# Who evicts the keys, and ScalarE's order, in the 48 rounds of a decoder's cross-attention

## What is computed

```python
k = at @ Wk.T + bk ; v = at @ Wv.T + bv        # at: 1500 x 256 for each batch entry, 16 heads of 16
scores = clip(q @ k.T / 4, -50, 50)            # masked rows: -50
ctx = softmax(scores) @ v
```

## Time and profile before

| what | value |
|---|---|
| median of 3 runs | 502.4 us |
| the profiled execution, its own time | 503.83 us |
| its span, first to last instruction | 502.0 us |
| TensorE busy | 475.0 us (95%) |
| VectorE busy | 363.7 us (72%) |
| ScalarE busy | 322.2 us (64%) |
| mean granted TensorE clock | 0.993 |

### The profile page before, as it was taken

One profiled execution on the slowest core, in us unless ns is written; L12 is line 12 of the kernel. 1 busy time (PEld: TensorE's weight loads), 2 busy tenths in 40 slices (PEclk: granted clock), 3 DMA queues, 4 the chain that ended last, 5 costly groups with the idle time before them and its releaser, 6 DMA issues.

```text
span 502.0 us, 16406 instructions
## 1 busy us (share of the span) xinstructions
PE 475.0 (95%) x7067; PEld 406.5 (81%) x7067; DVE 363.7 (72%) x817; ACT 322.2 (64%) x594; POOL 4.2 (1%) x15
## 2 busy tenths in 40 slices
PE   8999999999898999999999999899999899986897
PEld 7999999998787888888878878778878787674575
DVE  5666887788566755567956678965878965797973
ACT  4777787778563666567666567666666656445744
POOL 1000000000000000000000000000000000000000
PEclk9999999999998999999999999999999999998999
DMA  6466441202301221111111111111111100000000
GB/s 198 143 233 249 153 154 48 63 23 98 134 5 41 50 72 51 43 43 43 43 44 43 44 43 43 44 42 44 43 44 44 43 3 3 3 1 0 1 10 28
DMA packets 12236, 30.86 MB, mean 61 GB/s; under 512 B 1666, under 2 KB 4867, under 8 KB 11396
## 3 DMA queue, kind: packets, MB, share of 16 engines
q1 hardware_dynamic: 11716, 29.08, 18.4%
q0 software_dynamic: 192, 0.51, 0.3%
q10 hardware_dynamic: 256, 0.23, 0.1%
HBM read 29.35 MB, written 0.46 MB: 59 GB/s over the span
## 4 chain that ended last, share of the span: by engine, by line
PE 73%; DVE 15%; ACT 6%; issue 4%; DMA 1%; DVEq 0%; SPq 0%; ACTq 0%
PE psb L1438 12%; PE psb L1428 11%; PE psa L1499 9%; PE psa L1347 7%; PE psb L1517 7%; PE psa L1360 4%; PE pst L1369 3%; PE psb L1400 3%; PE psa L1380 2%; ACT shared L625 2%; PE psa L1759 1%; PE pst L1584 1%; DVE st L777 1%; PE psb L1391 1%; DVE shared L993 1%
## 5 line engine op out<-in xcount | busy, mean ns | idle before, releaser
L1438 PE MATMUL psb<-wkv,cx 128*125 128x256 f32 x576 | 80.4, 288 | 5.5 <-ACT kx L463 5.5
L1438 PEld LDWEIGHTS psb<-wkv,cx 128*125 128x125 f32 x576 | 71.0, 186 | 8.1 <-ACT kx L463 6.6
L1428 PE MATMUL psb<-cx,wkv 128*128 128x500 f32 x276 | 74.6, 405 | 0.2 <-ACT vmem L470 0.2
L470 ACT ACTIVATE vmem<-psb 125x512 f32<-125x512 f32 x45 | 26.8, 596 | 55.1 <-PE psb L1438 55.1
L1428 PEld LDWEIGHTS psb<-cx,wkv 128*128 128x128 f32 x276 | 48.3, 188 | 12.0 <-ACT vmem L470 0.3
L1499 PE MATMUL psa<-qb,kx 32*125 32x112 f32 x1536 | 55.7, 282 | 0.8 <-ACT shared L625 0.6
L1499 PEld LDWEIGHTS psa<-qb,kx 32*125 32x125 f32 x1536 | 47.2, 186 | 8.3 <-issue 3.7
L993 DVE TENSOR_SCALAR shared<-shared,top 125x896 f32<-125x896 f32 x48 | 30.8, 684 | 31.6 <-ACT shared L625 31.3
L625 ACT ACTIVATE smem<-psa 125x1792 f32<-125x1792 f32 x23 | 38.3, 1667 | 14.3 <-PE psa L1499 14.3
L993 DVE TENSOR_SCALAR smem<-smem,top 125x896 f32<-125x896 f32 x48 | 30.8, 683 | 21.8 <-ACT smem L625 21.2
L625 ACT ACTIVATE shared<-psa 125x1792 f32<-125x1792 f32 x24 | 40.0, 1666 | 10.4 <-PE psa L1499 10.1
(11 more groups left out here) (341 smaller groups left out, 830.3 us busy)
## 6 DMA issues: line engine op xcount, KB each, us to landing
ring<-ctx_t_dram SPq DMA_DIRECT2D x24, 500.0 KB, 3.5
whd<-wqk_dram SPq DMA_DIRECT2D x16, 256.0 KB, 2.7
qb<-wvp_dram SPq DMA_DIRECT2D x8, 256.0 KB, 2.9
whd<-wo_dram SPq DMA_DIRECT2D x16, 128.0 KB, 2.7
wraw<-w_dram SPq DMA_DIRECT2D x2, 1024.0 KB, 5.9
mats_sb<-mats_dram SPq DMA_DIRECT2D x1, 1536.0 KB, 10.0
wraw<-gate_dram SPq DMA_DIRECT2D x1, 1024.0 KB, 6.7
wraw<-up_dram SPq DMA_DIRECT2D x1, 1024.0 KB, 7.2
```

The source lines that it names most:

```text
L470: nc.scalar.activation(vu[u % 2][:, 2 * r:2 * r + 2, :, 0:XD], bank[0:CT, :].rearrange("p (t h d) -> p t h d", t=2, d=XD), ACT.Copy).then_ ...
L1428: last = nc.tensor.matmul(bank[:, 0:UT], wkv[a][:, 0, c, m * P:(m + 1) * P], cx[b][u % 2][:, c, :], start=(a == b and c == 0), stop=(a == ...
L1438: last = nc.tensor.matmul(bank[0:CT, t * D:(t + 1) * D], cx[b][u % 2][:, c, a0:a0 + CT], wkv[a][:, 1, c, :], start=(a == b and c == 0), st ...
```

## The change

It has five parts.

1. Keys. `move_k` stays on ScalarE in odd rounds from 3, but for 17, 29 and 41 (`BEHIND`). A new `take_k` on VectorE evicts them in every even round from 2, after that round's `early` steps and before its `clip`, and in 17, 29 and 41 after `remainder` and before the `early` steps. TensorE's waits stay.
2. ScalarE's order. `move_xnT` comes before `round_up`; a new group `first` stands there too, with `root(2)` (was in the round before), `move_y2` (was in the round before) and `root(5)` (was in the round before); `root(3)` goes from early to late.
3. VectorE's order. `add_delta` goes from before `clip` to behind it, `quantise_hidden` from behind `weigh` to between `clip` and `weigh`.
4. The tail. `root(5, 3)` goes ahead of the table load for `gelu(2)`; `hidden_part(1)` goes ahead of `hidden_part(2)`; the additions and the two stores that follow them change places to match.
5. The opening of TensorE: 6 of the matmuls of ones in fp32, 8 in fp32r, and 16 with 32 rows each.

```diff
+BEHIND = (17, 29, 41)
 # ScalarE
+            def first(t, o):
+                if o == 2:
+                    root(2, t)
+                if o == 8:
+                    move_y2(t)
+                if o == 14:
+                    root(5, t)
             def late(t, o):
-                if o == 1:
-                    root(2, t)
+                if o == 2:
+                    root(3, t)
-                if o == 7:
-                    move_y2(t)
-                if o == 13:
-                    root(5, t)
                 exponential(s)
-                if s >= 2 and u + 1 < B * UPB:
+                if r and s > 1 and s not in BEHIND and u + 1 < B * UPB:
                     move_k(u + 1, r, kvb)
+                if s in (2, 4, 6):
+                    move_xnT(s // 2)
+                for t in reversed(range(NT)):
+                    first(t, s - 12 * (t + 1))
                 if r == 0 and s not in SILU and u + 2 < B * UPB:
                     round_up(u + 2)
-                if s in (2, 4, 6):
-                    move_xnT(s // 2)
             move_aT(3)
+            root(5, 3)
             nc.scalar.preload_act_table(ACT.Gelu_apprx_tanh)
             gelu(2)
             back()
-            root(5, 3)
 # VectorE
+            def take_k(u, m):
+                dve.wait_ge(s_kp, 2 * u + m + 1)
+                dve.wait_ge(s_qk, 2 * u - 2)
+                nc.vector.tensor_scalar_add(kx[u % 2][:, m, :], kvb[:, 0:UT], cols_sb[:, 1, m:m + 1]).then_inc(s_ke, 1)
+            def between(t, o):
+                if o == 2:
+                    add_delta(t)
+                if o == 8:
+                    quantise_hidden(t)
                 if s % 2 and s // 2 + 2 < B * UPB:
                     remainder(s // 2 + 2)
+                if s in BEHIND:
+                    take_k(s // 2 + 1, 1)
...
                     early(t, s - 12 * (t + 1))
+                if s % 2 == 0 and s and s // 2 + 1 < B * UPB:
+                    take_k(s // 2 + 1, 0)
                 clip(s)
+                for t in reversed(range(NT)):
+                    between(t, s - 12 * (t + 1))
                 weigh(s // 2, s % 2)
...
+            last_add(1)
+            normalise7(3)
             last_add(2)
-            normalise7(3)
-            last_add(1)
 # TensorE
-            for _ in range(18):
+            rounded = ones.bitcast(F32R)
+            for _ in range(6):
                 nc.tensor.matmul(T0[:, 0:P], ones[:, :], ones[:, :], start=True, stop=True)
+            for _ in range(8):
+                nc.tensor.matmul(T0[:, 0:P], rounded[:, :], rounded[:, :], start=True, stop=True)
+            for k in range(16):
+                g = 32 * (k % 4)
+                nc.tensor.matmul(PS[k % 4][:, 0, 0:TT], rounded[g:g + 32, :], rounded[g:g + 32, 0:TT], start=True, stop=True, tile_position=(g, 0))
...
-            hidden_part(2, 0)
-            hidden_part(2, 1)
             pe.wait_ge(s_z, 6)
             hidden_part(1, 0)
             hidden_part(1, 1)
+            hidden_part(2, 0)
+            hidden_part(2, 1)
```

More of the change, by code:

```diff
@@ L295, in _ @@
                 sp.dma_start(ctxs[u % 3], ctx_t[u]).then_inc(s_ctx[u % 3], 16)
-            for i, t in enumerate((0, 2, 1, 3)):
-                sp.wait_ge(s_fin, i + 1)
+            for t in range(NT):
+                sp.wait_ge(s_fin, t + 1)
                 sp.dma_start(out[t * TT:(t + 1) * TT, :], xs[:, t, :]).then_inc(s_out, 16)
@@ L583, in early @@
                     move_ctxT(t)
-                if o == 2:
-                    root(3, t)
                 if o == 3:
@@ L1165, in last_add @@
             def last_add(t):
-                dve.wait_ge(s_fo, (1, 3, 2, 4)[t])
+                dve.wait_ge(s_fo, t + 1)
                 nc.vector.tensor_tensor(xs[:, t, :], xs[:, t, :], bank_fo[t][0:TT, 0:D], ALU.add).then_inc(s_fin, 1)
@@ L1173, in early @@
                     centre_delta(t)
-                    add_delta(t)
                 if o == 4:
@@ L1200, in late @@
                     scale_hidden(t)
-                if o == 8:
-                    quantise_hidden(t)
                 if o == 9:
```

## The result

The changed kernel takes 517.1 us (median of 4 runs, 515.66 to 518.39), the kernel before in the same comparison 501.6 us (4 runs, 500.69 to 503.15): a ratio of 1.031, 95% interval 1.028 to 1.033. A later comparison of the same two kernels gave 516.5 us (6 runs) and 1.029 (1.026 to 1.032). The change costs about 15 us (14.6 and 15.5 by the two pairs of medians). The forecast was 514.1, with 506 to 518 as its range.

A forecast was written before the change was run, and what follows sets the result against it. TensorE, busy 95% of the span, was taken to bound the kernel. Rounds +6.3 (losses 16.3 less gains 10.0), clock +4.8 and tail +0.6 gave +11.7 on 502.4: 514.1 us, range 506 to 518.

The forecast's parts named there:

- The place of the key: VectorE's key slot behind three butterflies in rounds 18, 30, 42: TensorE waits 2.3, 3.0 and 3.0 us, together 8.4.
- Rival C: Keys of the even rounds are in time, VectorE having 28% idle: 494.3 us; chance 0.12, of which 0.04 no change.
- The price of a key: One key's eviction on VectorE: 0.68 us, and 0.05 to TensorE, with no surcharge for reading PSUM.
- The clock: A fall of the clock behind each wait of rounds 18, 30, 42: 3 x 1.6 = 4.8 us, bounds 0 and 6.
- Rival B: Same waits in rounds 18, 30, 42, but the clock holds behind all or two: 509.3 to 511 us; chance 0.26.
- The opening: Matmuls of ones before the first projections end sooner, data come as before: 0 taken, bound 1.6 to 3.2 us.
- Rounds 2 and 3: xnT no longer stands behind `round_up`: `project_k` of round 3 at 155.5, 3.4 us gained, about 0.4 us of waiting left.
- Rival D: In the first rounds the wait moves whole from xnT to the values' eviction: 517.5 us; chance 0.06.
- Steps 0, 2, 4, 5, 8: Rounds 12/24/36 lose 1.3 us, 14/26/38 2.4, 28/40 2.4; 29/41 lose 1.8, gain 3.4; 20/32/44 gain 2.3.
- The cover elsewhere: The ring's loads, issued behind `weigh` up to 2 us later, still land with time to spare but for round 2.
- The tail: The root behind the table loads for `gelu(2)` starts at 487.4 instead of 486.85; last tile's chain ends 0.6 us later.
- rival E: The shorter opening leaves the first projections at half clock: +3, 517 us; chance 0.04.

The follow-up runs named there:

- e1: The changed kernel with the keys of rounds 18, 30 and 42 on ScalarE again: 504.6 us, 1.006 to the kernel before.
- e5: The changed kernel with the keys of rounds 18, 30 and 42 still on VectorE but ahead of the `early` steps: 506.6 us, 1.009 to the kernel before.
- e7: The kernel before with only the keys of every even round from 2 on VectorE ahead of `clip`: 514.9 us, 1.026.
- e3: The changed kernel with 8, 12 and 12 unused bf16 matmuls in TensorE's waits of rounds 18, 30 and 42: 512.6 us, 1.022 to the kernel before.
- e2: The changed kernel with the old opening of 18 fp32 matmuls of ones: 514.7 us, 1.026 to the kernel before.
- e4: The kernel before with the new opening alone: 504.2 us, 1.007.
- e6: The kernel before with `move_xnT` ahead of `round_up` in rounds 2, 4 and 6, nothing else: 499.6 us, 0.995.
- e10: The kernel before with the new tail alone: 501.8 us, 0.999.
- e8: The kernel before with `move_xnT` first, rounds 20, 32, 44 reordered with keys on VectorE, and the keys of 29, 41 on VectorE: 497.7 us, 0.990.

## Why the prediction was right, and where it was not

**The place of the key.** Right, and shown from both sides: e1 takes three keys away from VectorE, e5 leaves them there and moves them up, and either gives back 10 us or more. e7 adds that the even keys alone, on the kernel before, make a loss of nearly the same size, though spread otherwise over the rounds. The working that gave it was to compare two times, VectorE's slot and TensorE's arrival, round by round. It gave 2.3, 3.0 and 3.0 us for waits of 2.41, 2.88 and 2.88, and 1.2 and 0.9 for waits of 1.26 and 0.61. Rival C, whose rule is that VectorE has 28% idle time, fails in the same rounds: the idle time lies elsewhere.

**The price of a key.** 0.74 us on VectorE (18.4 over 25) against 0.68 taken, 0.05 to TensorE as taken. Mis-sized by 0.06, with little weight in the sum. ScalarE took 0.67 us for the same eviction (30.9 over 46 in the kernel before), so VectorE is slower at it by 0.07, too little to matter.

**The clock.** Right in kind, and e3 isolates it: 3 to 4 us by the ratios. A fall cost 1.3 to 1.7 us in the traces, where the forecast took 1.6. Wrong in one step: I took 2.21 us of waiting as enough for a fall, since the earlier trace rows had one behind it. In the changed kernel the wait of 2.41 us had none and the two of 2.88 had one each, in both of its traces and in e2's. Rival B (the clock holds behind some) was thus partly true in the traced execution, in one place of three. The other bound, that a wait of 1.7 us has none, does not hold either: e4 has half clock behind one of 1.69, while e7 has full clock behind waits of 1.89, 1.95 and 1.84. What sets off a fall is not told by the length of the wait alone, so a term for it is a chance times a price.

**The opening.** Wrong: the term was 0, the measured 2.5 us in the traces and 3.5 (2.3 to 4.7) alone. The step that failed is "they end sooner, and the data come when they did. Nothing gained". It asked only when the data come, while the 18 matmuls had a second use, that TensorE entered its first projections at full clock. Its upper bound, 3.2 us, holds the value of the traces and not the middle of e4's interval. Whether the kind of matmul (fp32r, 32 rows), their shorter time or the longer idle behind them (1.04 to 2.20 us in the six traces with the new opening, 0.35 and 0.42 in two with the old one) brings the half clock was not separated.

**Rounds 2 and 3.** Right: the time, 3.4 us against 4.0 in the changed kernel and 3.7 to `project_k` of round 3 in e6, and the rest of the wait, 0.4 against 0.38. Rival D, that the wait moves whole, is refuted by e6. The 3.4 and 4.0 are measured against a trace in which these rounds were slow; against e10's trace, in which they were fast, e6 gains about 1 us up to round 4.

**Steps 0, 2, 4, 5, 8.** Each within 0.6 us. They rest on the same comparison of two times.

**The cover elsewhere.** Wrong, at no cost: the ring's loads were said to land with time to spare but for round 2. In the kernel before `round_up` of round 30 waits 0.86 us for its context already, and in the changed kernel's trace four besides that of round 2 wait, in rounds 12, 18, 30 and 42: 0.19, 0.49, 1.48 and 3.55 us. TensorE paid 0.2 us for it there; in e1 and e8, where it comes earlier to round 43, it paid 1.19 and 0.96 in that round.

**The tail.** The forecast's 0.6 was 0.3 in the traces, most of it there before `root(5, 3)` starts, and e10 shows that the edit costs nothing that can be told. The wait for the tables was counted rightly, and what VectorE would do meanwhile was not looked at. The Trainium skill ("ScalarE: Activation LUTs", What ACT_TABLE_LOAD costs) counts some 2.7 us for a switch with its drain. In ScalarE's timeline of the changed kernel a switch takes its 1.28 us and no more:

```profile
495.65 1.28 ACT L712 ACT_TABLE_LOAD   x1
496.95 0.95 ACT L580 ACTIVATE qb<-qb 128x896 f32<-128x896 f32 x1
497.92 1.28 ACT L515 ACT_TABLE_LOAD   x1
499.21 0.29 ACT L333 ACTIVATE lnv<-mv,eps 112x1 f32<-112x1 f32 x1
```

The gaps between these four are 0.02 us or less: the rows bear out 1.28 and show no drain beside it, and the sum was right to go by them.

**From the traced execution to the median.** This is why 514.1 was 3.0 us under 517.1. The sum was worked out on an execution of the kernel before that was 1.4 us above the median and had a fall of the clock, and was then added to the median; and the changed kernel's traced execution was 1.5 us below its own median. Between the two spans the forecast was 11.7 for 11.8, and that this agrees so closely is luck: the opening's +2.5 was missed, and terms forecast too high (rounds 2 and 3 by 0.6, step 5 by 0.6, the clock by 1.4, the tail by 0.3) made up for it. Without the new opening the change would have cost about 9 us by the traces and 13 by e2's median. The measured 517.1 is also the figure that the prediction gave rival E.

Open: what decides, from execution to execution, whether the clock falls. The difference between e2's gain (1 to 2 us) and the opening's price in e4 (2.3 to 4.7) lies behind round 0, since both traces have 2.5 us up to there.

## What to carry to other kernels

Before work is moved to an engine with idle time, compare for each place the start of its slot in that engine's order with the arrival of the one who waits, and look first at the rounds where the engine's longest chain stands ahead of the slot; 3 of 25 places carried 12 of 15 us here, and a place further up in the order, ahead of two butterflies, took 10 of them away. Matmuls that compute nothing may be there for the clock: ask what the array does between them and the first real work, and what state it arrives in. Where the clock falls or a DMA lands late in some executions only, the difference of two traces isn't the difference of the medians, and each wait that is removed or made has a second price at a chance.

## What was not expected of the hardware

- Behind a wait of 2.41 us TensorE kept its full clock (12 matmuls in 1.67 us), behind two of 2.88 us it ran at half (2.70 and 2.92 us). In the kernel before a wait of 2.21 us was followed by half clock too, in e4 one of 1.69 us (2.44 us), and in e7 one of 1.95 us was not (1.68 us).
- With the new opening, which ended 1.6 us earlier in the changed kernel and 1.2 in e4, 12 fp32r matmuls of 448 columns took 4.82 and 4.85 us for 2.75.
- The column of the granted clock isn't to be trusted at the very start. In e1, and in e3 too, it reads 1.00 over a stretch in which the same 12 matmuls took 4.38 us (4.82 in e3), so the mean granted clock of such an execution is too high:

```profile
10.06 4.38 PE L1373 MATMUL psa<-cx 128*128 128x448 f32 x12 [0.72 <-ACT cx L363]
...
10.00:14.00 4.00, 3.94 (x11) 3.53 (x12) 2.44 (x5) 2.02 (x4) 0.00 (x0) 1.00 0.80 271
```
